# Last chunk's expert output on weighed rows: one attention output times sixteen weight rows, experts summed in PSUM in f32, one normalising pass at the end

## The reference, cut to what matters

```python
def moe_proj(p):
    y = jnp.einsum('nc,ech->neh', x, p)
    return jnp.einsum('ne,neh->nh', w, y)        # w: router weights, 16 experts
q, k, v = moe_proj(q_proj), moe_proj(k_proj), moe_proj(v_proj)   # reshaped (b, t, h)
scores = jnp.einsum('bth,bsh->bts', q, k) / sqrt(h)
attn = jax.nn.softmax(scores, axis=-1)
o = jnp.einsum('bts,bsh->bth', attn, v).reshape(n, h)
z = jnp.einsum('ne,nh->enh', w, o)
out = jnp.einsum('enh,ehc->nc', z, o_proj)       # all 16 experts, C = H = 128
...
x = x + out
```

## Time and profile before

| | |
|---|---|
| median of 3 runs | 533.54 us (532.94 to 533.87) |
| profiled execution, its own time | 532.82 us |
| its span | 531.0 us |
| PE busy | 445.4 us (84%) |
| DVE busy | 423.8 us (80%) |
| ACT busy | 241.4 us (45%) |
| mean granted PE clock | 0.937 of full |
| chain that ended last | PE 66%, DVE 26%, issue 5%, ACT 2% |
| output gathers, L1472 on DVE | 256 operations, 89.1 us, 350 ns each |
| output matmuls, L699 on PE | 192 matmuls, 51.7 us, 380 ns each |

### The profile page before, as it was taken

The page is one execution under the profiler, slowest core; times in us unless marked ns, Lnnn a source line. Parts: engine busy times, 40 slices in busy tenths (PEclk is TensorE's granted clock), DMA queues, the critical chain, the costliest instruction groups (busy, mean ns, idle before and its releaser), DMA issues.

```text
span 531.0 us, 8982 instructions
## 1 busy us (share of the span) xinstructions
PE 445.4 (84%) x3474; PEld 302.8 (57%) x3474; DVE 423.8 (80%) x883; ACT 241.4 (45%) x406; POOL 54.2 (10%) x69
## 2 busy tenths in 40 slices
PE   3999978999799969200799989999999999999653
PEld 1448968997258744100389975567555656555310
DVE  6989999886765659999825568756998998997987
ACT  5678736562472239883554753235223223321200
POOL 3050000000092006300180000000000000000000
PEclk9999989999799999755799988999999999999999
DMA  7991967910081004203320000069820000000000
GB/s 213 419 396 66 317 235 252 328 60 0 1 251 67 1 1 153 85 0 124 115 89 1 2 1 1 1 190 397 314 71 7 6 5 7 6 11 6 6 15 10
DMA packets 20353, 56.13 MB, mean 106 GB/s; under 512 B 2596, under 2 KB 5031, under 8 KB 20311
## 3 DMA queue, kind: packets, MB, share of 16 engines
q1 hardware_dynamic: 19872, 55.46, 30.0%
q10 hardware_dynamic: 438, 0.11, 0.1%
HBM read 53.36 MB, written 1.15 MB: 103 GB/s over the span
## 4 chain that ended last, share of the span: by engine, by line
PE 66%; DVE 26%; issue 5%; ACT 2%; DMA 0%; DVEq 0%; ACTq 0%
PE bk L654 15%; PE bk L662 8%; DVE XT L1472 7%; DVE QS L1240 5%; PE bk L365 5%; PE bk L699 5%; PE bk L387 4%; PE bk L360 4%; PE bk L595 2%; DVE RC L993 2%; PE bk L549 2%; PE bk L471 1%; PE bk L480 1%; PE bk L508 1%; DVE RA L1310 1%
## 5 line engine op out<-in xcount | busy, mean ns | idle before, releaser
L1472 DVE SCALAR_TENSOR_TENSOR XT<-bk,WK,XT 128x128 f32<-128x128 f32 x256 | 89.1, 350 | 8.8 <-PE bk L699 0.4
L654 PE MATMUL bk<-X,RB 128*128 128x512 f16 x384 | 94.9, 384 | 0.0
L910 ACT ACTIVATE X<-RA 128x512 f16<-128x512 f32 x64 | 40.1, 630 | 104.9 <-DVE RA L1487 83.5
L699 PE MATMUL bk<-RB,RA 128*128 128x512 f16 x192 | 51.7, 380 | 12.5 <-DVE XT L1472 9.8
L654 PEld LDWEIGHTS bk<-X,RB 128*128 128x128 f16 x384 | 36.7, 99 | 44.3 <-issue 4.5
L662 PEld LDWEIGHTS bk<-RB,X 128*128 128x128 f16 x768 | 48.9, 99 | 15.4 <-issue 0.6
L662 PE MATMUL bk<-RB,X 128*128 128x128 f16 x768 | 54.0, 220 | 0.0
L365 PE MATMUL bk<-X,RC 128*128 128x128 f16 x768 | 47.9, 219 | 2.0 <-DVE RC L993 1.8
L365 PEld LDWEIGHTS bk<-X,RC 128*128 128x128 f16 x768 | 45.2, 98 | 4.1 <-issue 3.4
L1460 DVE TENSOR_TENSOR X<-RA,X 128x512 f16<-128x512 f32 x64 | 43.8, 685 | 1.9 <-ACT X L910 1.9
L765 ACT ACTIVATE WK<-bk 128x512 f32<-128x512 f32 x48 | 28.6, 596 | 28.8 <-PE bk L365 20.8
(11 more groups left out here) (285 smaller groups left out, 774.1 us busy)
## 6 DMA issues: line engine op xcount, KB each, us to landing
RA<-in_wx SPq DMA_DIRECT2D x27, 768.0 KB, 5.9
RC<-expert_weights SPq DMA_DIRECT2D x22, 256.0 KB, 6.3
X<-in_w SPq DMA_DIRECT2D x8, 512.0 KB, 3.5
RC<-in_wx SPq DMA_DIRECT2D x5, 768.0 KB, 6.1
RC<-in_w SPq DMA_DIRECT2D x8, 384.0 KB, 4.2
STG<-in_w SPq DMA_DIRECT2D x6, 384.0 KB, 6.7
WBOT<-expert_weights SPq DMA_DIRECT2D x8, 256.0 KB, 6.6
STG<-expert_weights SPq DMA_DIRECT2D x6, 256.0 KB, 8.8
```

The lines of the kernel that those rows point to most:

```text
L654: t = e.matmul(BK[m][:, :], P16[:, wp, wo:wo + 128], ZH[:, n % 4, xp, :], start=(e1 == 0 and i == 0), stop=(e1 == 15 and i == 2))
L699: t = e.matmul(bank_o(n)[:, :], OT16[:, xp, bb_(4 * c + b)], P16[:, wp, 6144 + 512 * g:6656 + 512 * g], start=(i == 0), stop=(i == 2))
L910: e.activation(ZH[:, r, 0, :], zf[r], ACT.Copy).then_inc(S("z_hi"), 1)
L1472: stt(XT[:, bb_(t_)], bank_o(n)[:, bb_(i)], RW[:, t_, e1:e1 + 1], XT[:, bb_(t_)], ALU.mult, ALU.add).then_inc(S("acc"), 1)
```

## The change

For chunks 0, 1 and 2 nothing changes. For chunk 3:

- The residual is transposed at step 60 in place of step 68 (`attention[60] = (3, 3)`); the step loop ends with step 66, the last product.
- After the loop PE does: scores of chunk 3, output groups 43, 44, 45 (still chunk 2), the transposes of the exponentials, each waiting only for its own tile's exponentials, and the attention output into bank 4. No f16 halves of it are made.
- DVE multiplies the attention output (512 columns, read from bank 4) by each of the sixteen weight rows of chunk 3, `WR[16 + e1]`, into sixteen SBUF tiles `ZW`; chunk 2's gathers 45, 46, 47 stand after the second, fifth and eighth of these.
- PE multiplies each tile of `ZW[e1]` by the expert's output weights in f32 (`WO`, a new 1 MB load of `w2[:, 6144:8192]` into `WEFF`) and accumulates the sixteen experts of tile b in one bank: `BK_T` = banks 0, 1, 2, 5. Experts 0 to 11 go expert by expert, output groups 46 and 47 stand after experts 2 and 5, and experts 12 to 15 go tile by tile.
- DVE then does one operation per tile: bank times inverse sum plus residual, into `XT`, and SP stores the tile.
- On DVE, `gather(42)` now stands before the negative maximum of chunk 3, where before it stood behind it.
- On SP, the load of `WO` stands ahead of all output stores and waits for `weighed` 36 (the last use of `WEFF` as weight rows).

The core of the diff:

```diff
-        attention = {16 * c + LAG + 16 + d: (c, i) for c in range(4) for i, d in enumerate((0, 2, 4, 1))}
+        attention = {16 * c + LAG + 16 + d: (c, i) for c in range(3) for i, d in enumerate((0, 2, 4, 1))}
+        attention[60] = (3, 3)
         plan = {}
-        for c in range(4):
+        for c in range(3):
             for n in range(16):
                 plan.setdefault(16 * c + LAG + 21 + n, []).append((c, n // 4, n % 4))
-        STEPS = max(plan) + 2
+        STEPS = NI + LAG
         groups = [x for k in sorted(plan) for x in plan[k]]
+        WO = WEFF[:, :]
+        BK_T = (BK[0], BK[1], BK[2], BK[5])
+        ZW = [ZB[:, 512 * i:512 * i + 512] for i in range(4)] + [QT[:, 512 * i:512 * i + 512] for i in range(4)]
+        ZW += [STG[:, i // 3, 512 * (i % 3):512 * (i % 3) + 512] for i in range(6)] + [PK0T[:, 512 * i:512 * i + 512] for i in range(2)]
...
                 elif i == 1:
-                    q.wait_ge("exp", 4 * c + 4)
                     q.wait_ge("turned", c + 1)
                     for b in range(4):
+                        q.wait_ge("exp", 4 * c + (b + 1 if c == 3 else 4))
                         t = e.transpose(BK[5][:, bb_(b)], PP[:, bb_(4 * c + b)], pk1("ident"))
...
+            attend(3, 0)
+            for n in (43, 44, 45):
+                output(n)
+            attend(3, 1)
+            attend(3, 2)
+
+            def weighed_output(e1, b):
+                q.wait_ge("zw", e1 + 1)
+                q.wait_ge("wo", 16)
+                if e1 == 0:
+                    q.wait_ge(*(("qv_out", 8), ("k_out", 4), ("qv_out", 8), ("ptt", 4))[b])
+                return e.matmul(BK_T[b][:, 0:128], ZW[e1][:, bb_(b)], WO[:, bb_(e1)], start=(e1 == 0), stop=(e1 == 15), skip_group_check=True)
+
+            for e1 in range(12):
+                for b in range(4):
+                    weighed_output(e1, b)
+                if e1 in (2, 5):
+                    output(46 + (e1 == 5))
+            for b in range(4):
+                for e1 in range(12, 16):
+                    t = weighed_output(e1, b)
+                t.then_inc(S("tile"), 1)
...
+            softmax(3)
+            ptt(3)
...
+            gather(42)
+            negative_max(3)
+            gather(43)
+            gather(44)
+            inverse_sum(3)
+            for e1 in range(16):
+                q.wait_ge("otmm", 4)
+                q.wait_ge("zlo", NI)
+                q.wait_ge("qkvmm", 12)
+                tt(ZW[e1], BK[4][:, :], WR[16 + e1], ALU.mult).then_inc(S("zw"), 1)
+                if e1 in (1, 4, 7):
+                    gather({1: 45, 4: 46, 7: 47}[e1])
+            for b in range(4):
+                t_ = 12 + b
+                q.wait_ge("tile", b + 1)
+                q.wait_ge("rs", 4)
+                q.wait_ge("turned", 4)
+                stt(XT[:, bb_(t_)], BK_T[b][:, 0:128], RS[:, t_:t_ + 1], XT[:, bb_(t_)], ALU.mult, ALU.add).then_inc(S("done"), 1)
...
+            q.wait_ge("weighed", 36)
+            e.dma_start(WO, A["w2"][:, 6144:8192]).then_inc(S("wo"), 16)
             for c in range(4):
                 for b in range(4):
-                    n = groups.index((c, b, 3))
                     t_ = 4 * c + b
-                    q.wait_ge("acc", 4 * n + 4)
+                    q.wait_ge(*(("acc", 4 * groups.index((c, b, 3)) + 4) if c < 3 else ("done", b + 1)))
                     e.dma_start(out[bb_(t_), :], XT[:, bb_(t_)]).then_inc(S(f"out{c}"), 16)
```

More of the change, by code:

```diff
@@ L50 @@
      ("ffmm", 24), ("ffdown", 12), ("x3mm", 4), ("mlp_up", 16), ("prod_q", 60)),
-    (("down", 48), ("weffmm", 4), ("fwt", 3), ("ret_amm", 1), ("wbotmm", 8), ("zmm", 4), ("mlp_down", 16), ("prod_o", 64)),
+    (("down", 48), ("weffmm", 4), ("fwt", 3), ("ret_amm", 1), ("wbotmm", 8), ("zmm", 4), ("mlp_down", 16), ("prod_o", 48), ("tile", 4)),
     (("mean", 4), ("rstd", 4), ("vvmm", 4), ("turn0", 1), ("qkvmm", 12)),
@@ L60 @@
     (("route_exp", 2), ("theta", 1), ("q_sh", 4), ("sq", 4), ("rt_exp", 2), ("ptt", 4)),
-    (("x_hi", 4), ("wt16", 1), ("wts", 3), ("ot_hi", 4)),
+    (("x_hi", 4), ("wt16", 1), ("wts", 3), ("ot_hi", 3)),
     (("gated", 48), ("weff", 4), ("diag", 4), ("fw_lo", 3), ("sin", 32), ("k", 4), ("g", 8), ("x1", 4), ("l_max", 4), ("l_lo", 4),
-     ("ff_max", 24), ("gate16", 4), ("gated_ff", 4), ("ot_ff", 4), ("o_lo", 12), ("x2", 4), ("pp", 4), ("w2", 2), ("weighed", 64)),
+     ("ff_max", 24), ("gate16", 4), ("gated_ff", 4), ("ot_ff", 4), ("o_lo", 12), ("x2", 4), ("pp", 4), ("w2", 2), ("weighed", 64), ("zw", 16)),
     (("h_lo", 16), ("xg", 4), ("kadd", 4), ("l_hi", 4), ("g2_max", 4), ("gated16_0", 1), ("o_max", 4), ("o_hi", 12), ("x4", 4), ("zlo", 64)),
@@ L68 @@
     (("const", 2), ("sh_lo", 2), ("sim_sq", 1), ("ffs", 4), ("k_out", 4)),
-    (("x_lo", 4), ("xq", 4), ("quant", 12), ("ot_lo", 4)),
-    (("route", 29), ("router", 70), ("rw", 4)),
+    (("x_lo", 4), ("xq", 4), ("quant", 12), ("ot_lo", 3)),
+    (("route", 29), ("router", 70), ("rw", 3), ("done", 4)),
     (("chosen", 5), ("l1p", 1), ("relm", 1), ("cos", 32), ("p16", 8)),
@@ L688, in attend @@
                 else:
-                    q.wait_ge(*(("ptt", c) if c else ("wts", 3)))
+                    q.wait_ge(*((("ptt", c), ("wts", 3))[c == 0]))
                     for b in range(4):
@@ L900, in scalar, with softmax, ptt @@
                     e.activation(WT16, BK[1][0:32, :], ACT.Copy).then_inc(S("wt16"), 1)
+            def softmax(c):
+                q.wait_ge("nm", 2 * c + 2)
+                q.wait_ge("router", 2 * ROUTER)
+                for b in range(4 * c, 4 * c + 4):
+                    e.activation(PP[:, bb_(b)], BK[4][:, bb_(b - 4 * c)], ACT.Exp, bias=NM[:, b:b + 1], scale=ISC,
+                                 accum_out=SS[:, b:b + 1]).then_inc(S("exp"), 1)
+            def ptt(c):
+                q.wait_ge("pttmm", c + 1)
+                e.activation(PTT[:, cc(c)], BK[5][:, :], ACT.Copy).then_inc(S("ptt"), 1)
             for k in range(STEPS):
@@ L919, in scalar @@
                     if i == 1:
-                        q.wait_ge("pttmm", c + 1)
-                        e.activation(PTT[:, cc(c)], BK[5][:, :], ACT.Copy).then_inc(S("ptt"), 1)
+                        ptt(c)
                     elif i == 2:
@@ L928, in scalar @@
                 if k in attention and attention[k][1] == 0:
[L929 to L934, removed]
+                    softmax(attention[k][0])
                 if k >= LAG and k < NI + LAG and (k - LAG) % 16 == 15:
@@ L1472, in gather, with negative_max, inverse_sum @@
                     stt(XT[:, bb_(t_)], bank_o(n)[:, bb_(i)], RW[:, t_, e1:e1 + 1], XT[:, bb_(t_)], ALU.mult, ALU.add).then_inc(S("acc"), 1)
+            def negative_max(c):
+                sl = slice(4 * c, 4 * c + 4)
+                q.wait_ge("scores", c + 1)
+                red(NM[:, sl], four(BK[4][:, :]), X_AX, ALU.max).then_inc(S("nm"), 1)
+                q.wait_ge("nm", 2 * c + 1)
+                ts(NM[:, sl], NM[:, sl], -ISC, None, ALU.mult).then_inc(S("nm"), 1)
+            def inverse_sum(c):
+                sl = slice(4 * c, 4 * c + 4)
+                q.wait_ge("exp", 4 * c + 4)
+                e.reciprocal(RS[:, sl], SS[:, sl]).then_inc(S("rs"), 1)
             n = 0
@@ L1493, in vector @@
                 if k in attention and attention[k][1] == 0:
[L1494 to L1499, removed]
+                    negative_max(attention[k][0])
                 if k - 1 in attention and attention[k - 1][1] == 2:
@@ L1504, in vector @@
                     tt(OT16[:, 1, cc(c)], BK[4][:, :], OT16[:, 0, cc(c)], ALU.subtract).then_inc(S("ot_lo"), 1)
-                    q.wait_ge("exp", 4 * c + 4)
-                    e.reciprocal(RS[:, sl], SS[:, sl]).then_inc(S("rs"), 1)
+                    inverse_sum(c)
                     q.wait_ge("rs", c + 1)
```

## The result

The changed kernel takes 524.79 us (median of 4 runs, 524.59 to 525.76) against 533.52 before: ratio 0.9837, 95% interval 0.9825 to 0.9849, so 8.7 us faster. The forecast was 524.0. Its profiled execution took 525.76, the longest of the four, with a span of 524.0.

What follows compares the result with a forecast made beforehand. DVE's gathers set the end, behind chunk 3's serial chain. Removing 64 gather operations (25 us) and 0.8, adding 9.6 of weighing, short waits and a 3.7 PE tail takes the span from 531.0 to 521.5: median 524.0, range 521.3 to 528.0.

Steps and rivals of the forecast that it cites:

- Step 60: Chunk 3's residual transposes put where PE paces the step loop: everything after moves by +0.45 us.
- The new order of gather 42: Gather 42 ahead of chunk 3's negative maximum: 1.52 of the 1.97 us by which the maximum starts later.
- Reading PSUM: Sixteen DVE weighings at 0.60 us, 9.6 in all, no price for PSUM; the skill's cycles give 0.66 each.
- f32 products: PE's expert products: 0.112 us an instruction, 0.89 an expert's four tiles, 14.3 for sixteen experts.
- DVE's waits of 0.8: DVE waits about 0.8 us before each of gathers 46 and 47 for PE's output groups.
- the terms of handing over: DVE start to PE 0.74 us, about 0.85 with an f32 weight load first; output group start to gather 0.85.
- the prediction's own signs of being wrong: Granted clock 0.50 after 495, f32 pitch above 0.12, a wait for `WO`, or step 60 longer by over 0.5.
- Rival 1: PE has little work after group 45; clock halves for 9.2 us, 3 to 4.6 on the path: 527.8; chance 0.14.
- that row: Earlier clock averages, 0.64 over 313 to 315 and 0.65 over 321 to 325, read as a 9.2 us fall.
- The argument against the rival: At half load with 0.8 us gaps, also after PE's idle time of 3.19, the clock had stayed at 1.00.
- Rivals 2 and 3: Half clock through the whole weighing, 537.0, chance 0.04; no waits at groups 46 and 47, 521.4, chance 0.08.

Runs made afterwards that it cites:

- at full clock (with fillers): Changed kernel plus ten f16 matmuls of 512 columns, results unread, in PE's idle time between output group 45 and the first f32 product: 523.66 us.
- combined version: Changed kernel with maximum before gather 42, residual turned behind the scores, groups 46 and 47 early, gathers 45, 46, 47 behind weighings 5, 10, 15: 519.88 us.
- the three with fillers: Unread f16 matmuls added to the changed kernel (523.66 us), to its form with f16 products (520.93) and to the combined version (520.12).
- the late load: Changed kernel with the load of the output weights waiting for the last weighing (64) in place of the 36th: 525.56 us.

## Why the prediction was right

The time lay in the range, 0.8 from the forecast (that it came so near is partly luck, see below), and the mechanism was the forecast one: gathers of chunk 3 gone from DVE, PE and DVE handing over expert by expert, PE the limit from expert 8 on. Starts, in us from the copy of k:

| | forecast | changed kernel, profiled | at full clock (with fillers) |
|---|---|---|---|
| maximum of chunk 3 | 3.73 | 3.64 | 3.64 |
| first exponential | 4.66 | 4.56 | 4.56 |
| first weighing | 8.60 | 9.25 | 8.33 |
| gather 46 | 13.95 | 15.44 | 13.53 |
| gather 47 | 18.10 | 19.44 | 17.54 |
| weighing 8 | 19.66 | 20.87 | 18.97 |
| last normalising | 27.85 | 29.06 | 27.15 |
| end of the span | 30.3 | 31.48 | 29.60 |

- Step 60: 0.45 forecast, 0.45 measured. The cost buys nothing: placed behind the scores instead, the transposes and the copy delay nothing.
- The new order of gather 42: 1.52 forecast, 1.42 on the chain. About 0.6 of that reaches the first weighing.
- Reading PSUM: six weighings take 3.67 with the last one's end, a pitch of 0.60. The Trainium skill's dearer cycles for PSUM operands (VectorE: DVE Perf Modes, The TRN2 errata), by the estimate 0.66 each, are not seen.
- f32 products: 32 instructions in 3.74 us in the combined version, 0.112 a piece with the last one's end taken off: right. DVE's waits of 0.8 were 0.70.
- Mis-sized: the terms of handing over. Without the clock the sum was 0.7 too long. Ahead of the first weighing 0.27 was too much, of it 0.09 up to the maximum and 0.11 for the attention output, which reaches its reader after 1.19 and not 1.30. The rest is gathers: one followed by other work takes 1.42 and not 1.56 (three times 0.14). DVE's result reaches an f32 product after 0.75 and not 0.85, but that gained nothing: from the end of gather 45 to the start of gather 46 it was 2.58, forecast 2.59.
- Missed: the clock. The forecast kept it at 1.00 and gave its fall 0.14. It fell in both profiled executions of the changed kernel, for 6.8 and 3.4 us, and in those with the maximum first, the residual late, groups 46 and 47 early, f16 products and the late load; in the three with fillers and in the combined version it did not fall before the last product. A clock of 0.50 after 495 was one of the prediction's own signs of being wrong. Rival 1 named the place and the cause, that PE had only four transposes and the attention output between group 45 and the first product, but its price of 3 to 4.6 was too high: it took a fall as long as in the earlier trace rows, and less of it was on the path. It also misread that row: 0.65 over 321 to 325 puts the return near 323.8 and not 322.8, so that fall lasted 10.2 us and not 9.2, and by its own working the price would have been higher still. The fall here cost 0.7 to 1.9, and the forecast's 0.7 of excess hid the smaller of these. The total was nearer than its parts, which is luck. The argument against the rival was weak: it compared PE's share of busy time, 50% in the earlier trace rows, where wide f16 matmuls filled that share; the changed kernel was 69% busy in 496 to 499, with one output group and four transposes spread over 1.29 us. And the idle time of 3.19 that it named was that of the weight loads; PE's own was 2.70:

```profile
502.19 1.47 PE L699 MATMUL bk<-RB,RA 128*128 128x512 f16 x6 [2.70 <-DVE RA L1504]
```

- Rivals 2 and 3 did not come: the clock returned after the first experts, and the waits at groups 46 and 47 stayed until the groups were moved.

The Trainium skill has a kernel whose clock goes up and down while it turns through PSUM banks, and puts it down to PE's small idle times between the groups (TensorE: Matmul & The Clock Gate, "A second HAM failure mode: psum-queue depth-cycling"). The runs agree as far as they go: turning through banks alone does not bring the clock down. With f32 products the clock came back while they turned through four banks and stayed. With f16 products, which leave PE idle between experts, it came back and fell again; with a matmul behind each expert from the third to the twelfth, and the time ahead filled, the same products in the same banks ran at 1.00.

## What to carry to other kernels

When per-tile gathers on DVE set the end, weighing the input of the experts' products, all four tiles in one operation, and letting PSUM sum the experts moves the work to an engine that idles, even at f32's price. Then the order of hand-overs decides: give the new bound engine a lead (work that the other engine waits for goes first). The combined version was another 4 us faster; in the profiles 3.4 us of that are order (27.15 to 23.71, both at full clock) and 0.45 the residual. And look at what PE does in the few us ahead of its new work: it may start that work at half clock.

## What the runs showed of the hardware that was not expected

The granted clock fell near 499.5 although no wait of PE listed between 492 and that moment was over 0.7 us: 496 to 499 shows 2.07 us of busy PE out of 3. Few, narrow matmuls with gaps went before it, and ten matmuls of 512 columns put between them kept it at 1.00. And making PE's work cheaper can keep it slow: f16 products ran at half clock for 10.2 us, and again at the end, where the f32 products came back to full clock after 3.4 to 6.8 and stayed. What exactly the clock follows no run here separates.
